# GpSimd adds the weighted expert rows of 23 mixtures, TensorE turns the sums with four transposes instead of eight

## The chip, the cores and the metric

The kernel runs on one core of a Trainium2 chip, in one launch. The metric is the device time of that core in microseconds. The reasoning below uses one profiled execution of the kernel before; how its time stands to the timed runs is in the table further down.

## What is computed

The input x has 64 sequences of 128 tokens with 256 channels; a context of the same length has 192 channels. In the reference, cut to what matters:

```python
x = x + xattn(layernorm(x), ctx)         # 16 heads of 64, softmax over 128 keys, projection with bias
h = layernorm(x)
probs = softmax(h @ gate_w.T)            # 8 experts
top2_w, top2_idx = top_k(probs, 2)
expert_out = silu(h @ expert_w[e].T + expert_b[e])         # for each expert e
mixed = sum over the token's two experts of top2_w * expert_out
x = x + mixed @ combine_w.T
```

All is float32. The change touches the sum in the line of `mixed`.

## The kernel before, in words

The 8192 tokens are 32 pairs of sequences, 256 tokens each. Time is laid out in slots, numbered s, eight to a pair (`SLOTS`); i = s // 8 is the pair and u = s % 8 the pair of heads that slot s works on. Each engine has its own loop over the slots (`for s, i, u in slots()`), and each executes its instructions strictly in the order written. The engines meet through semaphores.

Attention in one slot: TensorE turns the normalised probabilities of the head pair before (`turn_probs`, L607), makes queries and keys (`queries_keys`), then scores of the next head pair (`scores`), and after some general jobs `attend` and `project`, all through the helper `products` (L566), since each float32 product is three products of a high and a low part. ScalarE takes exponentials (`exps`, L828) and rounds PSUM results to their high parts (`split_hi`, L801). VectorE makes row maxima (L1008), sums and their inverses (L1015, L1017) and the low parts (L960). GpSimd splits the attended rows (`split_attended`, L1318 and L1320), normalises the probabilities by the inverse sums (`normalise_probs`, L1309), and does small work and the indirect DMAs (`scatter` L1328, `gather` L1341).

Experts: for the first 28 pairs (`SPARSE`) the tokens are sorted by expert in DRAM in five chunks. A block of 128 sorted rows is turned (`turn_block`, L690), multiplied by its expert's weights (`expert`) and stored to `sorted_y`. The last four pairs go through all experts after the attention phase (`dense`).

A mixture m is the last step for pair m. GpSimd gathers its four 128x256 row blocks (two tokens halves t by two experts k) into the buffer `got[m % 2]`, one indirect DMA each. At slot s in `plan.mix` ScalarE multiplies each block with its weights (`weigh`, L896). In slot s+1 TensorE runs the job `turn_mixed`: for each of the four 128x128 pieces of the result two transposes that accumulate in PSUM, so that the sum over the two experts is made there (`turn_sum`, L657). ScalarE and VectorE split the result (`mT_s`), and in slot s+2 TensorE multiplies it by the combining weights (`combine`). VectorE adds the kept x (L1037), and SyncE stores the result.

The order around the change is written out by `Plan`. In each slot TensorE does turn_probs, the early jobs (turn_block), queries_keys, scores, the mid jobs (value products, turning and gating of the pair, turn_mixed), attend, project, the late jobs (expert, combine). ScalarE does exps, pT, attended, tanh, early, qk, mid (where the high part of the turned mixture is taken), and last `weigh`. GpSimd does split_attended, normalise_probs, small work, scatter, gather. The attention phase is slots 0 to 255; a mixture is gathered over the two or four GpSimd slots just before it is weighed. Of the 28 mixtures of the sorted pairs, 23 are weighed at slots below 256; those before the end of attention stand at u = 7 and u = 1. The buffer `got` is free again when the turn of the mixture two before is made, which `gather` waits for.

The turn in `turn_sum` reads piece (t, k) of the buffer:

```python
for k in range(2):
    mm = pe.matmul(bank[:, a * N2 + t * P:a * N2 + (t + 1) * P],
                   src[:, 2 * t + k, a * P:(a + 1) * P], ident[:, :], is_transpose=True,
                   start=k == 0, stop=k == 1)
```

Of the kernel before, what the change touches and what calls it, by code (L numbers as in the profile page):

```python
# [5 lines left out]
P = 128  # L6
# [4 lines left out]
ALU = mybir.AluOpType  # L11
ACT = mybir.ActivationFunctionType
# [4 lines left out]
SLOTS = HEAD_PAIRS  # L17
# [38 lines left out]
class Plan:  # L56


    def __init__(self, pairs):
        self.ends = [sum(CHUNKS[:c + 1]) for c in range(len(CHUNKS))]  # L60
        self.blocks = [4 * n + 7 for n in CHUNKS]
        self.first = [sum(self.blocks[:c]) for c in range(len(CHUNKS))]
        self.chunk_of = [c for c, n in enumerate(CHUNKS) for _ in range(n)]

        self.turn, self.gather, self.mix = {}, {}, {}
        at = free = 0
        for c, end in enumerate(self.ends):
            at = max(at, SLOTS * (end + 1) + 6)
            for b in range(self.blocks[c]):
                self.turn[at] = (c, b, self.first[c] + b)  # L70
                at += 1
            free = max(free, at + 4)
            for m in range(end - CHUNKS[c], end):
                if m >= 2:
                    free = max(free, sorted(self.mix)[m - 2] + 1)
                for k in range(4):
                    while len(self.gather.get(free, [])) >= self.room(free, pairs):
                        free += 1
                    self.gather.setdefault(free, []).append((m, k))
                self.mix[max(free + 2, max(self.mix, default=0) + 2)] = m  # L80
                free += 1

        self.dense = {}
        at = SLOTS * pairs
        for n in range(DENSE_JOBS * (pairs - SPARSE)):
            m = SPARSE + n // DENSE_JOBS
            if n % DENSE_JOBS == 0:
                at = max(at, SLOTS * (m + 2))
            while len(self.dense.get(at, [])) >= (DENSE_PER_SLOT if at >= SLOTS * pairs + 2 else 2):
                at += 1  # L90
            self.dense.setdefault(at, []).append(n)
            if n % DENSE_JOBS == DENSE_JOBS - 1:
                free = at + 2
                while any(near in self.mix for near in (free - 1, free, free + 1)):
                    free += 1
                self.mix[free] = m

        self.pair_of = [self.mix[at] for at in sorted(self.mix)]
        self.turn_of = {m: r for r, m in enumerate(self.pair_of)}
        self.mix = {at: r for r, at in enumerate(sorted(self.mix))}  # L100
        self.last = max(max(self.turn) + 4, max(self.mix) + 4)
        self.jobs_at, order = {}, []
        for s in range(-SLOTS, self.last + 1):
            i, u = s // SLOTS, s % SLOTS
            early, mid, late = [], [], []
            for kind, k, off in ATTENTION_JOBS.get(u, []):
                if 0 <= i + off < (SPARSE if kind == "rank" else pairs):
                    mid.append((kind, (i + off) * per(kind) + k))
            if s in self.turn:
                early.append(("turn_block", self.turn[s][2]))  # L110
            if s - 1 in self.mix:
                mid.append(("turn_mixed", self.mix[s - 1]))
            if s - 1 in self.turn:
                late.append(("expert", self.turn[s - 1][2]))
            if s - 2 in self.mix:
                late.append(("combine", self.mix[s - 2]))
            self.jobs_at[s, "early"], self.jobs_at[s, "mid"], self.jobs_at[s, "late"] = early, mid, late
            order += early + mid + late
        self.place = {job: n for n, job in enumerate(order)}
        self.order = order  # L120
# [16 lines left out]
def xattn_moe_kernel(nc, x, ctxT, wq, wkv, wkv_rest, wproj, bproj, gateT, expertT, expert_b, combineT, out):  # L137
    pairs = x.shape[0] // (2 * P)
# [20 lines left out]
    with ExitStack() as stack:  # L159
# [3 lines left out]
        def sem(name):  # L163
            return stack.enter_context(nc.semaphore(name))
# [52 lines left out]
        def carve(n, rows):  # L217
# [117 lines left out]
            sem(n) for n in ("top_done", "route_step", "top_w_done", "hot_done", "rows_done", "blocks_done"))  # L335

        ctx_rest = sem("ctx_rest")
        ctx_lo, probs_done, weighted = (
            sem(n) for n in ("ctx_lo", "probs_done", "weighted"))
        eps_done = [sem(f"eps_done{n}") for n in (1, 2)]  # L340
        rstd_done = [sem(f"rstd_done{n}") for n in (1, 2)]

# [220 lines left out]
        def _(pe):  # L563
# [88 lines left out]
            def turn_sum(src, bank):  # L652

                for t in range(2):
                    for a in range(2):
                        for k in range(2):
                            mm = pe.matmul(bank[:, a * N2 + t * P:a * N2 + (t + 1) * P],  # L657
                                           src[:, 2 * t + k, a * P:(a + 1) * P], ident[:, :], is_transpose=True,
                                           start=k == 0, stop=k == 1)
                return mm  # L660

# [71 lines left out]
            def general(s, position):  # L733
                for kind, n in plan.jobs_at[s, position]:
                    if (before := plan.before_in_bank(kind, n)) is not None:
                        pe.wait_ge(drained[before[0]], before[1] + 1)
                    bank = gen_ps[plan.bank(kind, n)]
                    if kind == "value":
                        mm = value(n, bank)
                    elif kind == "turn_x":  # L740
                        pe.wait_ge(xn_done, n + 1)
                        mm = turn(x_raw, bank)
                    elif kind == "turn_x1":
                        pe.wait_ge(xn2_done, n + 1)
                        mm = turn(xn2[n % 2], bank)
                    elif kind == "gate":
                        mm = gate(n, bank)
                    elif kind == "rank":
                        mm = rank(n, bank)
                    elif kind == "turn_block":  # L750
                        mm = turn_block(n, bank)
                    elif kind == "expert":
                        mm = expert(n, bank)
                    elif kind == "turn_mixed" and plan.pair_of[n] < SPARSE:
                        m = plan.pair_of[n]
                        pe.wait_ge(weighted, m + 1)
                        mm = turn_sum(got[m % 2], bank)
                    elif kind == "turn_mixed":
                        m = plan.pair_of[n] - SPARSE
                        pe.wait_ge(dense_added, 2 * DENSE_JOBS * (m + 1))  # L760
                        mm = turn(acc[m], bank)
                    else:
                        mm = combine(n, bank)
                    mm.then_inc(made[kind], 1)
# [32 lines left out]
        def _(act):  # L797
# [94 lines left out]
            def weigh(m):  # L892
                act.wait_ge(gathered[m % 2], 64 * (m // 2 + 1))
                act.wait_ge(top_w_done, m + 1)
                for k in range(4):
                    last = act.activation(got[m % 2][:, k, :], got[m % 2][:, k, :], ACT.Copy, scale=top_w[:, m, k:k + 1])  # L896
                last.then_inc(weighted, 1)

            def gate_exps(j):
# [387 lines left out]
        def _(pool):  # L1287
# [18 lines left out]
            def normalise_probs(j, p):  # L1306
                pool.wait_ge(inv_done, j * HEAD_PAIRS + p + 1)
                b = p % 2
                pool.tensor_tensor(probs[b][:, :, :], probs[b][:, :, :],  # L1309
                                   inv_sums[b][:, :].unsqueeze(2).broadcast_to([P, 4, P]),  # L1310
                                   ALU.mult).then_inc(probs_done, 1)
# [20 lines left out]
            def gather(m, k):  # L1332
                c = plan.chunk_of[m]
                through = plan.first[c] + plan.blocks[c]
                if k == 0:
                    for r in range(RING):
                        pool.wait_ge(y_stored[r], 16 * blocks_in_ring(r, through))
                    pool.wait_ge(y_rows_done, c + 1)
                    if m >= 2:
                        pool.wait_ge(made["turn_mixed"], plan.turn_of[m - 2] + 1)  # L1340
                pool.indirect_dma_start(  # L1341
                    out=got[m % 2][:, k, :], out_offset=None, in_=sorted_y[c],
                    in_offset=bass.IndirectOffsetOnAxis(ap=y_row_of[:, m, k:k + 1], axis=0)).then_inc(
                        gathered[m % 2], 16)

            for b in range(AHEAD):
                pool.memset(k_s[b][:, :, :, :].bitcast(F32), 0.0)
# [19 lines left out]
            for s, i, u in slots():  # L1367
# [4 lines left out]
                    split_attended(i, u - 2)  # L1372
                if now:
                    normalise_probs(i, u)
                if s in (-SLOTS + 1, 1):
                    rsqrt(i + 1, 0)
                if u == 6 and i >= 0 and exists(i + 2):
# [52 lines left out]
```

## Time and profile before

| what | value |
|---|---|
| timed runs | 1630.62 us median of 3 (1629.04 to 1634.59) |
| the profiled execution | 1637.44 us |
| its span, first to last instruction | 1635.4 us |
| TensorE matmul / weight loads busy | 94% / 90% |
| VectorE, ScalarE, GpSimd busy | 77%, 65%, 54% |
| granted TensorE clock, mean | 0.989 of full |

All times of single instructions are from the profiled execution, in microseconds from the start of its span. Busy shares are averages over the whole span; a timeline row shows one instruction, or several alike merged, with its start and duration and, in brackets, the idle time of its engine before it. PE is TensorE, DVE VectorE, ACT ScalarE, POOL GpSimd, PEld TensorE's weight loads. The tile `stage` in the rows is the scratch buffer that holds `got`, the probabilities and more.

### The profile page before, as it was taken

How to read it: one execution, taken by the hardware profiler on the slowest of the kernel's cores; microseconds unless marked ns; L12 is line 12 of the kernel's file. 1: busy time of each engine (PE TensorE's matmuls, PEld its weight loads, DVE VectorE, ACT ScalarE, POOL GpSimd, SP SyncE). 2: the span in 40 equal slices, each digit the busy share in tenths (PEclk: the TensorE clock that was granted, in tenths of full speed). 3: DMA queues.
4: the chain of work that ended last, by engine and by line, in shares of the span. 5: the costliest groups of instructions: out<-in, count | busy, mean ns of one | idle time of the engine just before them, and what ended most of it. 6: DMA issues, size and time to landing. Idle time of an engine off the chain costs nothing.

```text
span 1635.4 us, 39352 instructions
## 1 busy us (share of the span) xinstructions
PE 1537.0 (94%) x11891; PEld 1470.2 (90%) x11891; DVE 1264.0 (77%) x3135; ACT 1062.0 (65%) x2890; POOL 879.9 (54%) x1185
## 2 busy tenths in 40 slices
PE   4999999998999999999999999999999999999787
PEld 4899999998999999998999999899998998999675
DVE  5788888777888888877877888877778787776566
ACT  4766666665666766675767667666766666666433
POOL 4655555555545555576655545575656465644410
PEclk9999999999999999999999999999999999999999
DMA  6633333333577777344677667467777776877722
GB/s 226 203 85 91 92 91 92 91 91 95 173 216 223 223 217 210 101 123 128 201 224 227 204 213 217 135 188 226 230 227 211 220 229 198 248 218 216 273 64 78
DMA packets 179131, 286.99 MB, mean 175 GB/s; under 512 B 23575, under 2 KB 113900, under 8 KB 178668
## 3 DMA queue, kind: packets, MB, share of 16 engines
q1 hardware_dynamic: 168172, 255.11, 52.7%
q0 software_dynamic: 10752, 29.37, 5.8%
q8 instruction: 99, 1.62, 0.4%
q14 instruction: 108, 0.88, 0.2%
HBM read 155.66 MB, written 61.62 MB: 133 GB/s over the span
## 4 chain that ended last, share of the span: by engine, by line
PE 73%; DVE 10%; issue 6%; ACT 5%; POOL 4%; DMA 1%; SPq 0%; ACTq 0%; DVEq 0%; POOLq 0%
PE gen_ps L566 21%; PE qk_ps L566 15%; PE o_ps L566 9%; PE proj_ps L566 9%; PE s_ps L566 8%; PE pT_ps L607 6%; ACT stage L801 2%; PE gen_ps L690 1%; PE gen_ps L657 1%; PE gen_ps L665 1%; DMA k_s<-qk_s 1%; DVE sums L1015 1%; ACT v_s_hi L801 1%; POOL sorted_x L1328 1%; POOL stage L1309 1%
## 5 line engine op out<-in xcount | busy, mean ns | idle before, releaser
L828 ACT ACTIVATE stage<-s_ps,neg_max 128x128 f32<-128x128 f32 x1024 | 292.8, 371 | 105.8 <-DVE neg_max L1008 95.7
L1318 POOL CAST o_s_hi<-stage 128x256 fp32r<-128x256 f32 x256 | 102.2, 399 | 477.0 <-ACT stage L801 471.8
L1309 POOL TENSOR_TENSOR stage<-stage,inv_sums 128x512 f32<-128x512 f32 x256 | 266.8, 1042 | 15.9 <-DVE inv_sums L1017 15.9
L801 ACT CAST pT_s_hi<-pT_ps 128x512 fp32r<-128x512 f32 x256 | 150.9, 589 | 150.9 <-PE pT_ps L607 141.8
L566 PE MATMUL s_ps<-k_s,qk_s 128*128 128x256 f32 x1536 | 226.6, 283 | 4.1 <-DMA k_s<-qk_s 3.2
L1015 DVE TENSOR_REDUCE sums<-stage 128x4 f32<-128x512 f32 x256 | 172.9, 676 | 66.5 <-ACT stage L828 56.7
L960 DVE TENSOR_TENSOR pT_s_lo<-pT_ps,pT_s_hi 128x512 fp32r<-128x512 f32 x256 | 172.8, 675 | 56.0 <-ACT pT_s_hi L801 50.3
L960 DVE TENSOR_TENSOR qk_s<-qk_ps,qk_s 128x512 fp32r<-128x512 f32 x256 | 175.8, 687 | 41.8 <-ACT qk_s L801 39.0
L566 PEld LDWEIGHTS s_ps<-k_s,qk_s 128*128 128x128 f32 x1536 | 201.4, 191 | 4.9 <-DMA k_s<-qk_s 3.9
L1320 POOL TENSOR_TENSOR o_s_lo<-stage,o_s_hi 128x256 fp32r<-128x256 f32 x256 | 188.0, 734 | 21.1
L801 ACT CAST v_s_hi<-gen_ps 128x512 fp32r<-128x512 f32 x129 | 75.7, 587 | 177.2 <-PE gen_ps L566 173.3
L801 ACT COPY stage<-o_ps 64x256 f32<-64x256 f32 x512 | 188.4, 368 | 3.1
L566 PE MATMUL qk_ps<-xT_hi,wq_s_hi 128*128 128x256 f32 x512 | 166.7, 326 | 11.4 <-DVE wkvr_s_lo L971 6.5
L566 PE MATMUL o_ps<-pT_s_hi,v_s_hi 128*128 128x256 f32 x512 | 156.0, 305 | 22.4 <-DVE pT_s_lo L960 19.2
L1008 DVE TENSOR_REDUCE neg_max<-s_ps 128x4 f32<-128x512 f32 x256 | 174.4, 681 | 2.5 <-PE s_ps L566 2.5
L801 ACT CAST qk_s<-qk_ps 128x512 fp32r<-128x512 f32 x256 | 152.8, 597 | 24.8 <-PE qk_ps L566 18.2
L566 PE MATMUL proj_ps<-wproj_s_hi,o_s_hi 128*128 128x256 f32 x512 | 149.5, 292 | 12.5 <-POOL o_s_lo L1320 12.5
L607 PE MATMUL pT_ps<-ident,stage 128*128 128x128 f32 x1024 | 156.9, 276 | 2.2 <-POOL stage L1309 1.0
L566 PE MATMUL o_ps<-pT_s_lo,v_s_hi 128*128 128x256 f32 x512 | 145.2, 284 | 0.0
L566 PE MATMUL o_ps<-pT_s_hi,v_s_lo 128*128 128x256 f32 x512 | 145.2, 284 | 0.0
L566 PE MATMUL qk_ps<-xT_lo,wq_s_hi 128*128 128x256 f32 x512 | 144.5, 282 | 0.0
L566 PE MATMUL proj_ps<-wproj_s_hi,o_s_lo 128*128 128x256 f32 x512 | 143.9, 281 | 0.0
(358 smaller groups left out, 4706.1 us busy)
## 6 DMA issues: line engine op xcount, KB each, us to landing
w_block<-expert_table SPq DMA_DIRECT2D x147, 512.0 KB
k_s<-qk_s SPq DMA_DIRECT2D x512, 128.0 KB
stage<-sorted_x SPq DMA_DIRECT2D x147, 128.0 KB
sorted_y<-stage SPq DMA_DIRECT2D x147, 128.0 KB
x_raw<-in_x SPq DMA_DIRECT2D x32, 256.0 KB
c_raw<-in_ctxT SPq DMA_DIRECT2D x32, 256.0 KB, 3.3
stage<-in_x SPq DMA_DIRECT2D x32, 256.0 KB
x_kept<-x SPq DMA_DIRECT2D x32, 256.0 KB
```

Of the source, the lines that this page charges most:

```text
L566: mm = pe.matmul(out_ap, l, r, start=start and n == 0, stop=stop and n == len(terms) - 1, skip_group_check=skip)
L607: mm = pe.transpose(pT_ps[:, k * P:(k + 1) * P], probs[p % 2][:, k, :], ident[:, :])
L657: mm = pe.matmul(bank[:, a * N2 + t * P:a * N2 + (t + 1) * P], src[:, 2 * t + k, a * P:(a + 1) * P], ident[:, :], is_transpose=True, start ...
L665: mm = pe.transpose(bank[:, a * N2 + t * P:a * N2 + (t + 1) * P], src[:, t, a * P:(a + 1) * P], ident[:, :])
L801: last = act.copy(to, of)
L828: last = act.activation(probs[p % 2][:, k, :], s_ps[:, k * P:(k + 1) * P], ACT.Exp, bias=neg_max[p % 2][:, k:k + 1])
L960: last = dve.tensor_tensor(lo, of, hi.bitcast(F32), ALU.subtract)
L1008: dve.tensor_reduce(neg_max[p % 2][:, :], s_ps[:, :].rearrange("p (k n) -> p k n", k=4), AX_X, ALU.max, negate=True).then_inc(max_done, 1)
L1015: dve.tensor_reduce(sums[p % 2][:, :], probs[p % 2][:, :, :], AX_X, ALU.add).then_inc(sums_done, 1)
L1309: pool.tensor_tensor(probs[b][:, :, :], probs[b][:, :, :], inv_sums[b][:, :].unsqueeze(2).broadcast_to([P, 4, P]), ALU.mult).then_inc(prob ...
L1318: pool.tensor_copy(hi[:, :, :], o_full).then_inc(o_hi, 1)
L1320: pool.tensor_tensor(lo[:, :, :], o_full, hi[:, :, :].bitcast(F32), ALU.subtract).then_inc(o_lo, 1)
```

## The change

GpSimd adds, for the 23 mixtures weighed below slot 256, the two experts' weighted rows of each token, in one instruction over 128 partitions and 512 columns, in place, and raises the new semaphore `rows_added`. TensorE's turn_mixed for these mixtures waits for `rows_added` in place of `weighted` and uses the plain `turn` (L665 before, four transposes). The add stands in GpSimd's slot s+1, behind normalise_probs. The four gathered blocks lie in a new order in the buffer, so that the first experts' blocks of both halves are neighbours, and the second experts' too; the gather, the weighing and `turn_sum` follow that order. The other five mixtures of sorted pairs, and the four of the dense pairs, are turned as before.

```diff
+        early = [m for at, m in sorted(self.mix.items()) if at < SLOTS * pairs]
+        self.added_first = {m: n for n, m in enumerate(early)}
...
@@ turn_sum
-                                           src[:, 2 * t + k, a * P:(a + 1) * P], ident[:, :], is_transpose=True,
+                                           src[:, t + 2 * k, a * P:(a + 1) * P], ident[:, :], is_transpose=True,
...
@@ general, TensorE
-                        pe.wait_ge(weighted, m + 1)
-                        mm = turn_sum(got[m % 2], bank)
+                        if m in plan.added_first:
+                            pe.wait_ge(rows_added, plan.added_first[m] + 1)
+                            mm = turn(got[m % 2][:, 0:2, :], bank)
+                        else:
+                            pe.wait_ge(weighted, m + 1)
+                            mm = turn_sum(got[m % 2], bank)
...
@@ weigh, ScalarE
-                    last = act.activation(got[m % 2][:, k, :], got[m % 2][:, k, :], ACT.Copy, scale=top_w[:, m, k:k + 1])
+                    last = act.activation(got[m % 2][:, k // 2 + 2 * (k % 2), :], got[m % 2][:, k // 2 + 2 * (k % 2), :], ACT.Copy,
+                                          scale=top_w[:, m, k:k + 1])
...
@@ gather, GpSimd
-                    out=got[m % 2][:, k, :], out_offset=None, in_=sorted_y[c],
+                    out=got[m % 2][:, k // 2 + 2 * (k % 2), :], out_offset=None, in_=sorted_y[c],
...
+            def add_rows(m):
+
+                pool.wait_ge(weighted, m + 1)
+                first, second = (got[m % 2][:, k:k + 2, :].rearrange("p t c -> p (t c)") for k in (0, 2))
+                pool.tensor_tensor(first, first, second, ALU.add).then_inc(rows_added, 1)
...
@@ the loop over the slots, GpSimd
                 if now:
                     normalise_probs(i, u)
+                if s - 1 in plan.mix and plan.pair_of[plan.mix[s - 1]] in plan.added_first:
+                    add_rows(plan.pair_of[plan.mix[s - 1]])
                 if s in (-SLOTS + 1, 1):
                     rsqrt(i + 1, 0)
```

## Rows read from the trace of the kernel before

**Rows 1.** The page: busy time by engine, and the chain by engine.
```profile
PE 1537.0 (94%) x11891; PEld 1470.2 (90%) x11891; DVE 1264.0 (77%) x3135; ACT 1062.0 (65%) x2890; POOL 879.9 (54%) x1185
...
PE 73%; DVE 10%; issue 6%; ACT 5%; POOL 4%; DMA 1%; SPq 0%; ACTq 0%; DVEq 0%; POOLq 0%
```

**Rows 2.** Timeline of TensorE in slot 200: start, duration, engine, line, operation.
```profile
1156.25 1.03 PE L657 MATMUL gen_ps<-ident,stage 128*128 128x128 f32 x8
```

**Rows 3.** Timeline of GpSimd in slots 200 and 201.
```profile
1157.24 1.04 POOL L1309 TENSOR_TENSOR stage<-stage,inv_sums 128x512 f32<-128x512 f32 x1
1158.43 1.06 POOL L1328 DMA_INDIRECT sorted_x<-xn,row_of  x1 [0.16 <-issue]
1161.37 0.39 POOL L1318 CAST o_s_hi<-stage 128x256 fp32r<-128x256 f32 x1 [1.88 <-ACT stage L801]
```

**Rows 4.** Timeline of TensorE in slots 130, 202, 216 and 256.
```profile
728.56 1.03 PE L657 MATMUL gen_ps<-ident,stage 128*128 128x128 f32 x8
...
1171.82 1.03 PE L657 MATMUL gen_ps<-ident,stage 128*128 128x128 f32 x8
...
1265.91 0.43 PE L566 MATMUL o_ps<-pT_s_hi,v_s_hi 128*128 128x256 f32 x1 [2.56 <-DVE pT_s_lo L960]
...
1522.41 1.04 PE L657 MATMUL gen_ps<-ident,stage 128*128 128x128 f32 x8
1523.82 0.38 PE L566 MATMUL o_ps<-pT_s_hi,v_s_hi 128*128 128x256 f32 x1 [0.37 <-issue]
```

**Rows 5.** Timeline of GpSimd in slots 130, 202, 203, 216 and 256.
```profile
728.12 1.04 POOL L1309 TENSOR_TENSOR stage<-stage,inv_sums 128x512 f32<-128x512 f32 x1
...
1170.28 1.03 POOL L1309 TENSOR_TENSOR stage<-stage,inv_sums 128x512 f32<-128x512 f32 x1
1175.28 0.20 POOL L1302 TENSOR_TENSOR var_eps<-mv,eps 128x2 f32<-128x2 f32 x1 [3.97 <-DVE mv L984]
...
1265.36 1.04 POOL L1309 TENSOR_TENSOR stage<-stage,inv_sums 128x512 f32<-128x512 f32 x1 [1.98 <-DVE inv_sums L1017]
...
1524.22 0.74 POOL L1320 TENSOR_TENSOR o_s_lo<-stage,o_s_hi 128x256 fp32r<-128x256 f32 x1
```

**Rows 6.** Chain of waits in slots 200, 201, 216: start, length, what.
```profile
1156.41 0.87 PE gen_ps L657 x8
1157.29 0.71 PE o_ps L566 x6
...
1159.54 0.44 PE pT_ps L607 x4
...
1265.87 0.04 issue
1265.91 1.50 PE o_ps L566 x6
```

**Rows 7.** Single lines' instructions: count, nanoseconds least/median/most, first and last start.
```profile
L657 PE MATMUL gen_ps<-ident,stage x224: 270/272/474, 715.9 to 1617.6; 128*128 128x128 f32 x112
...
L1291 POOL TENSOR_TENSOR w_block<-stage,w_block x8: 1275/1293/1478, 33.7 to 68.4; 128x512 fp32r<-128x512 f32 x8
```

**Rows 8.** Timeline of ScalarE in slots 200 and 201.
```profile
1157.38 0.59 ACT L801 CAST mT_s_hi<-gen_ps 128x512 fp32r<-128x512 f32 x1 [0.22 <-PE gen_ps L657]
1158.69 1.14 ACT L828 ACTIVATE stage<-s_ps,neg_max 128x128 f32<-128x128 f32 x4 [0.73 <-DVE neg_max L1008]
```

**Rows 9.** Stretches: length, busy time by engine, granted TensorE clock, DMA share, GB/s.
```profile
1263.40:1265.90 2.50, 0.00 (x0) 0.00 (x0) 2.36 (x10) 0.59 (x1) 0.54 (x1) 1.00 0.02 5
1266.50:1269.40 2.90, 2.90 (x16) 2.90 (x15) 2.52 (x7) 1.14 (x4) 1.06 (x1) 0.50 0.43 138
1613.30:1615.30 2.00, 0.00 (x0) 0.00 (x0) 1.96 (x5) 2.00 (x5) 0.00 (x0) 1.00 0.45 131
1615.40:1619.30 3.90, 2.49 (x20) 2.25 (x20) 2.77 (x5) 0.61 (x2) 0.00 (x0) 1.00 0.15 54
713.40:1521.70 808.30, 776.12 (x6174) 751.33 (x6175) 628.57 (x1574) 543.19 (x1510) 458.33 (x604) 0.99 0.70 208
```

More of the change, by code:

```diff
@@ L337, in xattn_moe_kernel @@
         ctx_rest = sem("ctx_rest")
-        ctx_lo, probs_done, weighted = (
-            sem(n) for n in ("ctx_lo", "probs_done", "weighted"))
+        ctx_lo, probs_done, weighted, rows_added = (
+            sem(n) for n in ("ctx_lo", "probs_done", "weighted", "rows_added"))
         eps_done = [sem(f"eps_done{n}") for n in (1, 2)]
```

## The prediction

> **What bounds the kernel now.** I read the page first, then the groups by line, then the timelines of single slots and the chain of waits. The page gives TensorE 94% of the span and GpSimd 54%; the chain that ended last runs 73% through TensorE and 4% through GpSimd [rows 1]. So work taken from TensorE in the attention phase is worth its full time there, and GpSimd has room on average. Whether it has room at the moment in question is another matter, and only a timeline tells.
>
> A mixture weighed by ScalarE in slot s is turned by TensorE in slot s+1. I number slots as the kernel does; 23 mixtures have s under 256. By the plan their turns fall into slots with u = 0 (12 of them: 128, 136, 144, 152, 192, 200, 208, 216, 232, 240, 248, 256) and u = 2 (11: the slot two behind each of these but the last). Slot 200 is a typical u = 0. There TensorE starts the eight turns at 1156.25 [rows 2], while GpSimd is still splitting; its normalisation of the same slot's probabilities runs from 1157.24 to 1158.28 [rows 3]. In a u = 2 slot TensorE has a value product ahead of the turn and comes later: in slot 202 it turns at 1171.82, and the normalisation ended at 1171.31 [rows 4, 5].
>
> **The change, step by step.**
>
> *Turns.* The eight transposes stand in the chain with 0.87 us, four probability transposes of the same shape with 0.44 [rows 6]. Four fewer save 0.43 us, and 23 x 0.43 = 9.9 us is all that the change can give. (The 272 ns of a single one [rows 7] overlap with the next and must not be summed.)
>
> *The add.* Nothing in the trace is this add. The nearest row is a 128x512 subtraction with two full inputs on GpSimd, 1293 ns in the median of 8 and 1478 at most [rows 7]; from below the normalisation, 128x512 with a broadcast second input, 1.04 us [rows 3]. I take 1.29, the shape and inputs being the same, and keep 1.04 and 1.48 as ends. The Trainium skill, "GPSIMD Engine Reference", section on elementwise cycle accounting, gives 4497 ns for such an add of 2048 columns and holds that elementwise work is better left to VectorE; a quarter of that is 1.12 us, an estimate, and with it the sum below would be some 4 us smaller. No run here shows the add yet.
>
> *Its place.* GpSimd executes in order and the add stands right behind the normalisation of its slot. Its own inputs are ready long before (the weighing was done before that slot's exponentials), so it starts 0.03 us before the normalisation is recorded as ended, and TensorE follows some 0.05 after its end (such a step between engines is 0.04 on the chain [rows 6]): turns start at normalisation end + 1.31 us. That new wait is the heart of the matter.
>
> *Slots with u = 0, eight alike* (128, 144, 152, 192, 200, 208, 240, 248). In slot 200: 1158.28 + 1.31 = 1159.59 instead of 1156.25, 3.34 us late [rows 2, 3], less 0.43 is 2.9. Over the eight I read 3.24 to 3.51 in the same way, mean 3.37, net 2.94: 23.5 us. Behind the waiting turn on TensorE are attend, project, the expert block and the whole next slot. In slots 200 and 201 there is no idle time in which to win it back. On ScalarE the rounding of the turned sums stands ahead of the next exponentials: it ended at 1157.97 and the exponentials began at 1158.69 [rows 8], so they slip too, and VectorE and GpSimd behind them. All four engines are held by one wait, and nobody runs ahead.
>
> *Slots 136, 216, 232* (u = 0 at a chunk's end). VectorE is busy with the list of blocks, and attend already waited: in slot 216 it began at 1265.91 [rows 4]. The normalisation ended at 1266.40 [rows 5]; turns at 1267.71, attend 0.44 later at 1268.15, 2.2 us later than now. Three of them: 6.7 us.
>
> *Slot 256* has no normalisation. The split ended at 1524.96 [rows 5], the add 1.26 later, turns at 1526.27, attend at 1526.70 instead of 1523.82 [rows 4]: 2.9 us. The gather behind it on GpSimd waits for this turn as well and slips by less than that.
>
> *Slots with u = 2.* Slot 202: 1171.31 + 1.31 - 1171.82 = 0.80, less 0.43: 0.37 us. Nine alike: 3.3. Slots 130 and 138 have no expert block's transposes ahead: 729.16 + 1.31 - 728.56 = 1.91, net 1.48 [rows 4, 5]; two: 3.0.
>
> *GpSimd itself.* 23 x 1.29 = 30 us more, hidden: in slot 200 it next splits at 1161.37, 3.1 us after the normalisation [rows 3]; in slot 202 it idles from 1171.31 to 1175.28 until VectorE's statistics come [rows 5]. One scatter issue of 1.06 us moves back into that room [rows 3]. Were the cover gone, each add would delay the next split by up to 1.3 us. ScalarE's weighing and the gathers only change which rows they address: nothing.
>
> Waits net of saved turns: 23.5 + 6.7 + 2.9 + 3.3 + 3.0 = 39.4 us.
>
> *The clock.* TensorE idles in each u = 0 slot for 3.2 us (1156.41 [rows 6] to 1159.59). In the trace an idle stretch of that size is followed by a stretch at half clock (1.2 instead of 2.4 GHz): after TensorE's idle 1263.4 to 1265.9 the granted clock is 0.50 for some 3 us, while an idle 2.0 us near 1614 leaves it at 1.00 [rows 9]. All eight idle stretches from 2.45 us up, the start aside, did this, and none below 2.2. The price is in slot 216: six attend matmuls cost 1.50 us on the chain instead of 0.71 [rows 6], projection and expert lose 0.57 and 0.42 likewise, 1.8 us in all. Nine new falls (eight alike and slot 256) cost 9 x 1.8 = 16 us; slots 136, 216 and 232 pay it already.
>
> Sum: 39.4 + 16 = 55 us. The profiled execution took 1637.4 us (span 1635.4), 6.8 above the median of the runs, 1630.6. On the median: 1630.6 + 55 = 1686.
>
> **Rivals.**
>
> *No fall of the clock.* If the new idle stretches do not bring it down, because they are cut by the few matmuls around them, only the waits stand: 1630.6 + 39 = 1670. For it: 3.2 us lies within, not above, the stretches that show a fall. Against it: 2.5 us was enough in slot 216 [rows 9]. Chance 0.23.
>
> *A longer cold stretch.* Around 765 the low clock lasted twice as long as elsewhere; if wait and fall meet so in most of the twelve slots, some 1.8 x 12 = 21 us come on top: 1707. Chance 0.10.
>
> *Recovered waits.* TensorE has 808 - 776 = 32 us of idle time between 713 and 1522 us [rows 9]. If the other engines use the stall to get ahead, up to that much returns: near 1654. Against it stands ScalarE's place behind the same turn. Chance 0.09.
>
> *Faster.* If the sum is there before TensorE asks, the change gives its 9.9 us: 1621. The place is the turn, the price the end of the add against the start of the turn; it decides once the normalisation ends 1.31 us before the turn. In u = 2 it ends 0.51 before, in u = 0 2.03 after, so none of the 23 qualifies. It needs the timeline to be wrong by microseconds. Chance 0.03, with 0.02 for something that cancels out.
>
> *It doesn't do what it says.* The four rows are gathered to new places, first rows in halves 0 and 1, second in 2 and 3, so one add yields the sums that four transposes turn; the later mixtures keep their eight. I see no way in which the adds fail to happen.
>
> **How the numbers follow.** My forecast with the clock's fall has 0.53, giving 1686, with the add's ends (23 x 0.25 less, 23 x 0.19 more) 1680 to 1691. The range reaches down to the recovered waits and up toward the long cold: 1653 to 1706. A measurement of this kernel tells some 0.3%, 5 us, from no change. Slower has 0.95, same 0.02, faster 0.03.
>
> **What would show it.** In the profile after: 23 adds of 128x512 on GpSimd at about 1.29 us; the 224 transposes of sums cut to 92 in fours and 40 in eights; TensorE before the four-fold turns idle on GpSimd, some 3.2 us in u = 0 and 0.8 in u = 2, 45 to 55 us in all; ScalarE's rounding of the turned sums waiting as long; a mean granted clock a little lower, with half-clock stretches behind the u = 0 turns. I am wrong if that wait is a few microseconds in total, or if the stall is there and the following slots are shorter by it.

## The result, and the profile after

The changed kernel took 1689.5 us in the median of 4 runs (1684.2 to 1691.0), the kernel before, run beside it, 1632.6. The ratio is 1.0346 with a 95% interval of 1.0322 to 1.0369: slower by 57 us, where 1686 in a range of 1653 to 1706 was forecast. The profiled execution is the fastest of the four, 1684.2 us, with a span of 1682.4.

The page of the kernel after, the lines that answer to [rows 1]:

```profile
PE 1541.0 (92%) x11799; PEld 1470.5 (87%) x11799; DVE 1264.8 (75%) x3135; ACT 1059.5 (63%) x2890; POOL 906.0 (54%) x1208
...
PE 67%; POOL 9%; ACT 8%; DVE 8%; issue 7%; DMA 1%; ACTq 0%; SPq 0%; POOLq 0%; DVEq 0%
```

TensorE executes 92 matmuls fewer, as it should, and is yet busy 4 us longer: a part of its work ran at a lower clock. In the chain that ended last its share fell from 73% to 67%, and GpSimd's rose from 4% to 9%. The totals of waits say on what TensorE waited, and the single line says how long the add takes (ns, least/median/most):

```profile
PE gen_ps L668 <- POOL stage L1358: 55.1, 23, 5.7
PE proj_ps L569 <- POOL o_s_lo L1328: 12.5, 17, 1.0
PE o_ps L569 <- DVE pT_s_lo L968: 11.6, 16, 3.7
```
```profile
L1358 POOL TENSOR_TENSOR stage<-stage x23: 1257/1262/1273, 714.6 to 1571.5; 128x512 f32<-128x512 f32 x23
```

23 waits of the turn (L668) for the add (L1358), 55.1 us together, the longest 5.7: this wait did not exist before, and it heads the list by far. Slot 200, the timeline of TensorE after, answers to [rows 2]:

```profile
1175.38 0.88 PE L569 MATMUL s_ps<-k_s,qk_s 128*128 128x256 f32 x6
1179.37 0.63 PE L668 MATMUL gen_ps<-ident,stage 128*128 128x128 f32 x4 [3.11 <-POOL stage L1358]
1179.75 0.36 PE L569 MATMUL o_ps<-pT_s_hi,v_s_hi 128*128 128x256 f32 x1
```

and that of GpSimd, to [rows 3]:

```profile
1176.28 0.73 POOL L1328 TENSOR_TENSOR o_s_lo<-stage,o_s_hi 128x256 fp32r<-128x256 f32 x1
1176.96 1.04 POOL L1317 TENSOR_TENSOR stage<-stage,inv_sums 128x512 f32<-128x512 f32 x1
1177.96 1.26 POOL L1358 TENSOR_TENSOR stage<-stage 128x512 f32<-128x512 f32 x1
1179.38 1.05 POOL L1336 DMA_INDIRECT sorted_x<-xn,row_of  x1 [0.15 <-issue]
```

Split, normalisation and add stand one behind the other on GpSimd, and TensorE, which has ended its scores, takes up the turn 0.15 us after the add. ScalarE is held behind it, as the timeline of ScalarE shows (see [rows 8]):

```profile
1180.09 0.59 ACT L808 CAST mT_s_hi<-gen_ps 128x512 fp32r<-128x512 f32 x1 [3.19 <-issue]
1180.57 1.15 ACT L835 ACTIVATE stage<-s_ps,neg_max 128x128 f32<-128x128 f32 x4
```

In slot 202 (u = 2) the wait is short, compare [rows 4]:

```profile
1196.96 0.63 PE L668 MATMUL gen_ps<-ident,stage 128*128 128x128 f32 x4 [0.71 <-POOL stage L1358]
```

The clock in slots 200 and 201, in stretches as in [rows 9], and then the same stretch of the chain, as in [rows 6]:

```profile
1176.30:1179.30 3.00, 0.00 (x0) 0.00 (x0) 1.95 (x4) 0.60 (x2) 2.92 (x3) 1.00 0.86 233
1179.40:1181.50 2.10, 2.10 (x15) 2.10 (x16) 0.76 (x2) 1.41 (x5) 1.03 (x1) 0.74 0.82 271
1181.50:1184.50 3.00, 3.00 (x18) 3.00 (x18) 1.02 (x3) 0.41 (x2) 0.00 (x0) 0.61 0.17 57
1185.50:1188.00 2.50, 2.50 (x18) 2.28 (x18) 1.88 (x5) 1.46 (x5) 2.15 (x4) 1.00 0.80 294
```
```profile
1179.37 0.63 PE gen_ps L668 x4
1180.00 0.84 PE o_ps L569 x6
1180.84 1.28 PE proj_ps L569 x6
1182.12 1.49 PE gen_ps L569 x7
```

TensorE is idle for 3 us, then the granted clock falls to 1.2 GHz for a few microseconds, and projection and expert block take 1.28 and 1.49 us where at 2.4 GHz they take 0.71 and 0.83. The slot, from one turn of the probabilities to the next, grew from 5.76 to 9.95 us.

Measured in this way in both profiles, the eight like slots with u = 0 grew by 4.0 to 4.5 us each, 34 in all, and the slots behind them by 1 in all; the three chunk ends by 2.6 to 2.9, net of the slots behind them 8; nine slots with u = 2 by 0.45 each and slots 130 and 138 by 1.57, together 7. In slot 256 the turn waited 3.7 us, and TensorE's next long idle stretch begins 21.0 us after that slot's turn of the probabilities instead of 17.0: 4 more. That makes 54. The two profiled executions are only 47 us apart (spans of 1682.4 and 1635.4), since that of the kernel before is 6.8 us above its median and that of the kernel after the fastest of its four. The 7 us between stand where the change does nothing, half of them ahead of slot 128 or in slots that it leaves alone, half in the dense pairs, where in the profile after the clock stayed at 1.00 behind two idle stretches of 3.0 us that were each followed by a fall in the profile before. So a difference of a few microseconds between two single profiles says nothing by itself; below I go by slots.

### The profile page after: what moved, and what is told of

The parts are those of the page before. It is cut to its first block, busy times and chain, and to the rows that moved or that the text cites. A ratio compares the mean times of both kernels' runs of the same rounds, so it can differ in the third digit from the quotient of the medians.

```text
span 1682.4 us, 39191 instructions
## 1 busy us (share of the span) xinstructions
PE 1541.0 (92%) x11799; PEld 1470.5 (87%) x11799; DVE 1264.8 (75%) x3135; ACT 1059.5 (63%) x2890; POOL 906.0 (54%) x1208
## 4 chain that ended last, share of the span: by engine, by line
PE 67%; POOL 9%; ACT 8%; DVE 8%; issue 7%; DMA 1%; ACTq 0%; SPq 0%; POOLq 0%; DVEq 0%
PE gen_ps L569 19%; PE qk_ps L569 13%; PE proj_ps L569 9%; PE o_ps L569 9%; PE s_ps L569 7%; PE pT_ps L610 6%; ACT stage L808 3%; POOL stage L1317 2%; PE gen_ps L668 2%; POOL o_s_lo L1328 2%; POOL stage L1358 2%; PE gen_ps L693 1%; POOL o_s_hi L1326 1%; ACT stage L903 1%; ACT stage L835 1%
## 5 line engine op out<-in xcount | busy, mean ns | idle before, releaser
L569 PE MATMUL proj_ps<-wproj_s_lo,o_s_hi 128*128 128x256 f32 x512 | 146.6, 286 | 0.0
```

The source lines that it names most:

```text
L569: mm = pe.matmul(out_ap, l, r, start=start and n == 0, stop=stop and n == len(terms) - 1, skip_group_check=skip)
```

## The experiments

All ratios are to the kernel before, run on the same chip in the same comparison, 1630.4 to 1631.0 us there. "Worth x us" is a ratio times 1631.

**Four transposes without the add (e1, and again e10).**

```diff
-                            pe.wait_ge(rows_added, plan.added_first[m] + 1)
+                            pe.wait_ge(weighted, m + 1)
                             mm = turn(got[m % 2][:, 0:2, :], bank)
...
-                if s - 1 in plan.mix and plan.pair_of[plan.mix[s - 1]] in plan.added_first:
-                    add_rows(plan.pair_of[plan.mix[s - 1]])
```

> No add is made; TensorE turns only the first experts' rows of the 23 mixtures with four transposes and waits for the weighing as before, so the second experts' share is left out of them. Theory (the loss is TensorE's wait for the add, the saving is real): 4 x 23 transposes at 0.11 us come off the bound engine, 1632.6 - 9.9 = 1623 us. Rival (transposes were hidden, so nothing could be gained): 1632 to 1633.

Measured: 1626.9 us, ratio 0.9971 (0.9955 to 0.9988). The saving is real but half of what was expected, 4.7 us instead of 9.9. Since that is my term of the sum that the trace seemed to give most directly, it was run again:

> The same kernel as the first run (four transposes, no add, the second experts' share left out), timed again with more rounds, because it gained 0.29% with an interval from 0.12% to 0.45%, where 9.9 us would be 0.6%. If each four transposes are worth their whole 0.43 us: ratio 0.994. If part is given back in the slot behind, where projection then waits for GpSimd's split (0.15 us in the u = 3 slots of that run): 9.9 - 11 x 0.15, less the three chunk ends (1.3), 7 us, ratio 0.9957. If more is lost elsewhere: 0.997 or above.

Measured: 1627.6 us, ratio 0.9973 (0.9955 to 0.9991), 4.4 us. Both intervals exclude 9.9 us; both hold 7, at their edge. Slot by slot the profile of the first run shows where it goes. The u = 2 slots are shorter by 0.44 each, seven of the eight like u = 0 slots by 0.31 to 0.43 and slot 128 by 0.08, but nine of the eleven u = 3 slots are longer by 0.14 to 0.18. Together that is 6.2 us without the chunk ends, in the profile of e10 as well, and 6.2 lies within both intervals. In the u = 3 slots TensorE has come nearer to GpSimd. The timeline of TensorE in slot 203 of that run, then GpSimd's:

```profile
1171.06 0.28 PE L569 MATMUL o_ps<-pT_s_hi,v_s_lo 128*128 128x256 f32 x1
1171.41 0.38 PE L569 MATMUL proj_ps<-wproj_s_hi,o_s_hi 128*128 128x256 f32 x1
```
```profile
1169.05 1.07 POOL L1336 DMA_INDIRECT sorted_x<-xn,row_of  x1 [0.20 <-issue]
1170.13 0.41 POOL L1326 CAST o_s_hi<-stage 128x256 fp32r<-128x256 f32 x1
1170.62 0.74 POOL L1328 TENSOR_TENSOR o_s_lo<-stage,o_s_hi 128x256 fp32r<-128x256 f32 x1
```

Projection starts 0.35 us after the last attend matmul, where 0.12 is the usual step, since GpSimd's split ends at 1171.36, held back by the scatter before it. In slots 216 and 232 attend waits for VectorE in any case.

**Sixteen transposes (e11)**, the price from the other side.

```diff
-                            pe.wait_ge(rows_added, plan.added_first[m] + 1)
-                            mm = turn(got[m % 2][:, 0:2, :], bank)
+                            pe.wait_ge(weighted, m + 1)
+                            turn_sum(got[m % 2], bank)
+                            mm = turn_sum(got[m % 2], bank)
```

and no add, as above.

> The kernel before with the eight transposes of each of the 23 mixtures made twice (16), no add. The price of transposes from the other side: 8 more are 0.87 us on the chain. If TensorE is the bound in all 23 slots: 23 x 0.87 = 20 us, ratio 1.0123. Where VectorE holds the slot (three chunk ends) or others absorb some: 17 us, 1.0104. If each transpose is worth only the half that the first run showed: 10 us, 1.006.

Measured: 1648.1 us, ratio 1.0103 (1.0082 to 1.0124), 17 us for 184 transposes more, as expected where three chunk ends absorb theirs. By slots the eight more cost 0.83 to 0.89 us in each like slot and each slot with u = 2. So a transpose added costs its 0.11 us, and one removed gives less: on the side of removal the next limit is near.

**The wait with all eight transposes (e2).**

```diff
                             pe.wait_ge(rows_added, plan.added_first[m] + 1)
-                            mm = turn(got[m % 2][:, 0:2, :], bank)
+                            mm = turn_sum(got[m % 2], bank)
```

> As the changed kernel, add and wait in place, but TensorE keeps its eight accumulating transposes, so the second experts' rows count twice in these mixtures. Theory: the wait costs the same and the saving is gone, 1689.5 + 9.9 = 1699 us, with the same idle before the turns (about 55 us). Rival (the stall ends on something other than the add, so the transposes fit into it): 1690.

Measured: 1699.8 us, ratio 1.042 (1.0392 to 1.0447), 12 us above the changed kernel by the ratios and 10 by the times. TensorE's totals of waits in that run:

```profile
PE gen_ps L660 <- POOL stage L1358: 55.9, 23, 6.0
```

The same wait, 55.9 us against 55.1, and four transposes more behind each. Behind such a wait the four transposes are worth their whole 0.43 us: nine slots with u = 2 are 0.89 to 0.92 us longer than in the kernel before, where in the changed kernel they were 0.45 longer. The price of the wait is therefore not 57 but 67 to 69 us, of which the change gives 10 to 12 back.

One slot of this run bears on the clock. Slot 192, the turn and the stretch behind it:

```profile
1130.63 1.06 PE L660 MATMUL gen_ps<-ident,stage 128*128 128x128 f32 x8 [3.27 <-POOL stage L1358]
1130.70:1133.70 3.00, 3.00 (x27) 3.00 (x27) 1.17 (x4) 1.63 (x5) 0.99 (x1) 1.00 0.53 150
```

TensorE idled 3.27 us and the clock did not fall. The slot is 3.5 us longer than before, the other seven like slots of the run, each with a fall, are 4.6 to 6.1 longer. So the fall is likely behind such a wait, and not certain.

**The stall filled (e3)**, to tell the idle time from the clock.

```diff
+                            if s % SLOTS == 0:
+                                for _ in range(24):
+                                    pe.transpose(bank[:, 0:P], ident[:, :], ident[:, :])
                             pe.wait_ge(rows_added, plan.added_first[m] + 1)
                             mm = turn(got[m % 2][:, 0:2, :], bank)
```

> As the changed kernel, but in slots with u = 0 TensorE turns the identity 24 times (24 x 0.11 = 2.7 us) into the bank ahead of its wait; the bank is written over afterwards. The stall of 3.2 us stays, only filled. Theory (some 16 us of the loss are the half clock that follows the idle stretches): the granted clock stays at 1.00 behind the eight alike slots and slot 256, 1689.5 - 16 = 1673 us. Rival (the clock costs nothing because TensorE waits anyway): 1689, or a little more.

Measured: 1670.3 us, ratio 1.025 (1.0222 to 1.0277); against the changed kernel 0.0096 of ratio, 16 us. The filling and the stretch behind it in slot 200 of that run, timeline and stretches:

```profile
1171.30 2.78 PE L762 MATMUL gen_ps<-ident 128*128 128x128 f32 x24
1174.48 0.65 PE L668 MATMUL gen_ps<-ident,stage 128*128 128x128 f32 x4 [0.40 <-POOL stage L1361]
```
```profile
1174.50:1180.50 6.00, 6.00 (x49) 5.91 (x50) 3.11 (x8) 3.98 (x11) 2.24 (x4) 1.00 0.58 163
```

TensorE does useless work for 2.8 us, waits 0.4 for the same add, and the clock stays at 2.4 GHz behind it; the mean granted clock over the run is 0.993 against 0.982. The rival that had the clock cost nothing is out: 16 us hang on it, give or take some 6 by the two intervals, and 41 us of the loss stay when it is kept up. By slots the split is finer. The eight like slots are 2.8 to 3.1 us longer than before in this run, mean 2.95, where they were 4.0 to 4.5 longer, mean 4.30, in the changed kernel: the clock's fall costs 1.35 us in each, and some 0.13 in the slot behind, 12 us for the eight. Slot 256 gives 1.5 more by the measure used above. The rest stands at the chunk ends, which are shorter than in the changed kernel by 1.0 to 2.3 us. There the kernel before had its falls already, but in slots 216 and 232 of the changed kernel the slow stretch lasts twice as long. Slot 216 of the changed kernel:

```profile
1297.40:1300.40 3.00, 3.00 (x15) 3.00 (x16) 1.15 (x4) 1.63 (x5) 1.00 (x1) 0.50 0.62 146
1300.40:1303.20 2.80, 2.80 (x15) 2.80 (x15) 0.64 (x2) 0.00 (x0) 0.00 (x0) 0.50 0.84 311
```

With the filling, one of the three chunk ends has no fall and two have a short one. How much of this part is the change's and how much an old loss cannot be told apart: chunk ends that are made alike differ by as much from run to run (see e5).

**Only the u = 2 mixtures added (e5).**

```diff
-        early = [m for at, m in sorted(self.mix.items()) if at < SLOTS * pairs]
+        early = [m for at, m in sorted(self.mix.items()) if at < SLOTS * pairs and at % SLOTS == 1]
```

> The changed kernel, but only the 11 mixtures turned in slots with u = 2 are added on GpSimd; the 12 of u = 0 are turned with eight transposes, as before. Theory (the wait is the end of the add against TensorE's arrival, 0.7 us in nine of these slots and 1.8 in two): 9 x 0.4 + 2 x 1.5 = 6.6 us over the kernel before, which ran at 1631 in the last comparison: 1638 us. Nearly all of the 55 us belongs to u = 0. Rival (each add costs alike, 55 / 23 = 2.4 us): 1657 us.

Measured: 1640.1 us, ratio 1.0048 (1.0032 to 1.0063), 8 us, with 10.0 us of TensorE's waits for the add. Adds do not cost alike: the same instruction costs 0.7 us in one place and 4 in another. By subtraction, the twelve of u = 0 carry the other 49.

This run also makes its chunk ends as the kernel before does, and shows what a fall alone costs. Slot 216, where TensorE idled 2.50 us ahead of attend (2.56 in the kernel before [rows 4]), the stretch behind:

```profile
1270.10:1273.10 3.00, 3.00 (x26) 3.00 (x27) 2.63 (x8) 1.22 (x5) 1.40 (x2) 1.00 0.50 162
```

The clock stayed at 2.4 GHz, and the slot took 8.55 us instead of the 10.10 of the profile before, where it fell [rows 9]. The three chunk ends with the slots behind them are 3.0 us shorter here than in that profile, and 2.9 in e8, though nothing was changed in them. All differences at chunk ends that I give are to that slower profile.

**A second instruction before the release (e6).**

```diff
-                pool.tensor_tensor(first, first, second, ALU.add).then_inc(rows_added, 1)
+                pool.tensor_tensor(first, first, second, ALU.add)
+                pool.tensor_tensor(second, second, second, ALU.add).then_inc(rows_added, 1)
```

> The changed kernel, but GpSimd makes a second instruction of the same size (it doubles the second experts' rows, which nobody reads any more) before it releases TensorE. Theory: every wait grows by one add, 23 x 1.27 = 29 us, from 1689.5 to 1719, or somewhat more if the clock falls in slots with u = 2 too, where the idle time grows from 0.7 to 2.0 us. Rival (something later than the add ends the wait, or the stall is won back): under 1700.

Measured: 1720.0 us, ratio 1.054 (1.0521 to 1.056), 32 us above the changed kernel. The second instruction and TensorE's wait, from the views of its line and of the waits:

```profile
L1359 POOL TENSOR_TENSOR stage<-stage x23: 1032/1038/1042, 717.7 to 1607.8; 128x512 f32<-128x512 f32 x23
```
```profile
PE gen_ps L668 <- POOL stage L1359: 78.3, 23, 6.7
```

It has the same tile as both inputs and takes 1.04 us, not 1.27. The wait grew by 78.3 - 55.1 = 23.2 us, 1.01 for each; the time grew by some 8 more, and the mean clock fell from 0.982 to 0.968. Slots 194 and 202 (both u = 2) show what these 8 us are: the turn, then the stretch behind it.

```profile
1155.89 0.63 PE L668 MATMUL gen_ps<-ident,stage 128*128 128x128 f32 x4 [1.71 <-POOL stage L1359]
1155.90:1158.90 3.00, 3.00 (x26) 3.00 (x27) 1.60 (x5) 1.63 (x5) 0.00 (x0) 1.00 0.82 234
1216.80 1.09 PE L668 MATMUL gen_ps<-ident,stage 128*128 128x128 f32 x4 [1.71 <-POOL stage L1359]
1216.80:1219.80 3.00, 3.00 (x14) 3.00 (x15) 1.20 (x3) 1.63 (x5) 0.00 (x0) 0.50 0.82 223
```

After the same idle 1.71 us the clock stayed up in one and fell in the other. Of the nine slots with u = 2 that idle so, five fell and are 2.7 to 2.8 us longer than before, the four others 1.46; of slots 130 and 138 one fell. These six falls are 7.6 us, less 1.4 that the slots behind gave back.

**The add at the head of GpSimd's slot (e4).**

```diff
                 now, before, nxt = exists(i), exists(i - 1), exists(i + 1)
+                if s - 1 in plan.mix and plan.pair_of[plan.mix[s - 1]] in plan.added_first:
+                    add_rows(plan.pair_of[plan.mix[s - 1]])
                 if u < 2 and before:
                     split_attended(i - 1, 6 + u)
...
                 if now:
                     normalise_probs(i, u)
-                if s - 1 in plan.mix and plan.pair_of[plan.mix[s - 1]] in plan.added_first:
-                    add_rows(plan.pair_of[plan.mix[s - 1]])
```

> As the changed kernel, but the add stands at the head of GpSimd's slot s+1, before the split and the normalisation. In slots with u = 0 it would run from about 1155.3 to 1156.5 in the times of the kernel before, where TensorE asks at 1156.25; in u = 2 GpSimd idles there for 4 us. Theory (only the add's place behind the normalisation costs): wait 0.35 us in eight slots, none in u = 2, 23 x 0.43 saved, some 1.5 us lost in slot 256: 1628 us, between 1624 and 1632. Rival (an add on GpSimd costs by itself, by delaying splits and normalisations): over 1640.

Measured: 1636.4 us, ratio 1.0036 (1.0022 to 1.005). Moving three lines takes away 51 of the 57 us, which puts the loss on the place of the add and not on the add. TensorE's waits for it:

```profile
PE gen_ps L668 <- POOL stage L1358: 4.8, 10, 1.2
```

But it is 6 us slower than before and not 3 faster. By slots in the profiles, the u = 2 ones gain their 0.44 us. Slot 128 loses 1.0 us with a wait of 1.2. Of the chunk ends, slot 216 with the one behind it loses 2.3 and slot 232 loses 1.3, although their turns wait 0.16 and 0.14 us. The cause is on VectorE. The add on GpSimd in slot 216, the instruction of VectorE beside it, TensorE's attend, and the same instruction of VectorE in the kernel before:

```profile
1258.75 1.31 POOL L1358 TENSOR_TENSOR stage<-stage 128x512 f32<-128x512 f32 x1
1258.23 1.88 DVE L1169 TENSOR_TENSOR_SCAN rows_to<-rows_new,zeros 128x9 f32<-128x9 f32 x1
1264.91 0.58 PE L569 MATMUL o_ps<-pT_s_hi,v_s_hi 128*128 128x256 f32 x1 [4.08 <-DVE pT_s_lo L968]
```
```profile
L1161 DVE TENSOR_TENSOR_SCAN rows_to<-rows_new,zeros x5: 178/178/182, 396.1 to 1363.5; 128x9 f32<-128x9 f32 x5
```

A step of VectorE's list of blocks that takes 0.18 us took 1.88, until GpSimd's add was done. The same happened in slot 232 (1.86 us) and, with the step two further on, in slot 136 (1.95). So the list ends later, and attend, which waits for VectorE there, starts 1.4, 1.4 and 2.0 us later in these slots than before. Stretches of slot 216 in that run:

```profile
1262.00:1264.50 2.50, 0.00 (x0) 0.00 (x0) 2.33 (x11) 0.00 (x0) 0.14 (x1) 0.76 0.00 0
1265.00:1268.00 3.00, 3.00 (x14) 3.00 (x15) 2.62 (x8) 1.14 (x4) 1.45 (x2) 0.50 0.52 164
1268.00:1271.00 3.00, 3.00 (x20) 3.00 (x19) 0.89 (x3) 0.72 (x2) 0.00 (x0) 0.64 0.71 215
```

TensorE also idles longer before attend, 4.1 us instead of 2.6; the clock falls while it still idles and stays low behind it for most of 6 us, where the kernel before had some 3 [rows 9]. That this longer slow stretch is the rest of slot 216's loss fits, but no run tested it by itself.

**Head of the slot, u = 2 only (e8).** The two edits of e4 and e5 together.

> The add at the head of GpSimd's slot, and only for the 11 mixtures turned in slots with u = 2, where GpSimd idles for some 4 us; the 12 of u = 0 are turned with eight transposes as before. Theory: no wait anywhere, 11 x 0.44 us saved, about 0.15 given back in the slot behind as the run with the add at the head showed: 1631 - 3 = 1628 us. Rival (the saving is lost in the next slot): 1631.

Measured: 1630.8 us, ratio 0.9994 (0.9985 to 1.0003). No gain that can be told from nothing; the 3 us expected would be 0.998, just outside the interval.

**The add on VectorE (e7).**

```diff
+            def add_rows(m):
+                dve.wait_ge(weighted, m + 1)
+                first, second = (got[m % 2][:, k:k + 2, :].rearrange("p t c -> p (t c)") for k in (0, 2))
+                dve.tensor_tensor(first, first, second, ALU.add).then_inc(rows_added, 1)
...
                 now, before, nxt = exists(i), exists(i - 1), exists(i + 1)
+                if s - 1 in plan.mix and plan.pair_of[plan.mix[s - 1]] in plan.added_first:
+                    add_rows(plan.pair_of[plan.mix[s - 1]])
                 if now:
                     inverse(i, u)
```

and GpSimd's call of `add_rows` is gone.

> The add is made by VectorE instead of GpSimd, at the head of its slot s+1, ahead of the row sums, for all 23. There VectorE idles about 1 us while ScalarE takes the exponentials, and such an add should take it 0.7 us. Theory (the saving is real where the wait is hidden): no wait of TensorE in 20 slots; the three slots at a chunk's end, where VectorE is late anyway, lose 0.7 us each. The run with four transposes and no add gained 5 us, so 1631 - 5 + 2 = 1628 us, between 1622 and 1633. Rival (VectorE has no room, each add delays the sums by 0.7 us): 1631 - 5 + 16 = 1642.

Measured: 1629.1 us, ratio 0.9992 (0.9979 to 1.0005). TensorE's wait for it, from the view of waits:

```profile
PE gen_ps L668 <- DVE stage L1230: 8.1, 3, 3.1
```

Three waits, those of the chunk ends; in the other 20 slots none. That names the next step:

**The add on VectorE, chunk ends left out (e9).**

```diff
-        early = [m for at, m in sorted(self.mix.items()) if at < SLOTS * pairs]
+        early = [m for at, m in sorted(self.mix.items())
+                 if at < SLOTS * pairs and not (at % SLOTS == 7 and at // SLOTS in self.ends)]
```

> As the run with the add on VectorE, but the three mixtures turned at a chunk's end (slots 136, 216, 232), where VectorE makes the list of blocks and its add came late, keep eight transposes. Theory: these three adds each cost VectorE 0.7 us on the path (2 us in all) and give nothing, so 1629 - 2 = 1627 us, a ratio to the kernel before of 0.9975. Rival (nothing to gain there): 0.999.

Measured: 1624.0 us, ratio 0.996 (0.9937 to 0.9983), a gain of 6 us over the kernel before (3 to 10 by the interval), and the fastest version with the full computation. Its adds, from the view of the line:

```profile
L1231 DVE TENSOR_TENSOR stage<-stage x20: 682/693/693, 711.2 to 1509.8; 128x512 f32<-128x512 f32 x20
```

0.69 us each, in time that VectorE spent waiting for the exponentials (0.9 to 1.9 us in these slots of the kernel before; behind the add it still waits 0.3 or more), and nobody waits for them.

## Why the prediction was right, point by point

- *The wait for the add, 39.4 us net.* Right: e3 leaves 41 us when the clock is kept up, and the eight like slots are 2.95 us longer there, against 2.94 forecast. In slots with u = 2 it is 0.45 against 0.37 in nine, and 1.57 against 1.48 in two, and in slot 256 2.4 (e3) against 2.9. At the three chunk ends attend starts 2.5 to 2.6 us later, against 2.2.
- *Its cause, the place behind the normalisation.* Shown by e4, where the same add a few instructions earlier costs 6 us instead of 57, by e5 for the split by u, and by e6 for the slope. e4 also shows a price that the prediction did not have: an add of GpSimd beside VectorE's list of blocks holds VectorE up.
- *The clock, 16 us for nine falls.* The mechanism was right, the term a little large: 1.35 us in each like slot and 0.13 behind it instead of 1.8, some 13 us for nine; e3 as a whole shows 16, but a part of that belongs to the chunk ends. That eight of eight idle stretches from 2.45 us up brought a fall, and none below 2.2, held in the one trace it was read from, and not in others: slot 192 of e2 idled 3.27 us without a fall, slot 216 of e5 2.50 without one, and in e6 1.71 us were enough in five slots of nine. All nine new idle stretches of the changed kernel's profile were followed by a fall, so the count came true, but it was a likelihood and not a rule. The fall comes somewhat after the stall, during attend, so attend's first matmuls still run at 2.4 GHz; in slot 216 of before, from which the 1.8 was taken, it came at once.
- *The add, 1.29 us.* 1.26. The rows with two full inputs were the right ones, against the 1.04 with a broadcast input. The 1.12 that the prediction estimated is a quarter of the 4497 ns that the Trainium skill, "GPSIMD Engine Reference", section "Elementwise — side-by-side cycle accounting", gives for an add of 2048 columns. The trace of the kernel before has an instruction of that size, a subtraction, which agrees (4547 ns), but a quarter of the columns takes more than a quarter of the time (1262 ns):

```profile
L1291 POOL TENSOR_TENSOR wproj_s_lo<-stage,wproj_s_hi x1: 4547/4547/4547, 24.2 to 24.2; 128x2048 fp32r<-128x2048 f32 x1
```

- *Release to start, 0.05 us.* Wrong by 0.1: TensorE starts 0.14 to 0.15 us after GpSimd's add ends, in all 23 places. That is 2 us, of which the shorter add (23 x 0.03) takes back 0.7, and it is the 0.08 by which the u = 2 slots came out longer.
- *The saving, 9.9 us.* Right in the place where it counted, behind the wait: 10 to 12 us by e2 against the changed kernel. But the sentence that TensorE's work in the attention phase "is worth its full time there" is wrong for the kernel without the wait, where e1 and e10 gave 4.7 and 4.4 us. The give-back to GpSimd's split in u = 3 slots is seen (nine times 0.15 us, 1.4 in all), and the chunk ends give nothing for three of the 23; by slots that leaves 6.2 in both profiles without the chunk ends, and what is lacking to the timed 4.4 and 4.7 is within the intervals.
- *Recovered waits.* Did not come: the slots behind the eight like stalls were as long as before, or by up to 0.3 us longer. Rounding the turned sums stands ahead of the exponentials on ScalarE, as forecast, and holds the other engines.
- *A longer cold stretch.* Came in two places, slots 216 and 232, where the slow stretch lasted twice as long as before; it did not in the eight like slots.
- *The sum.* By slots the terms come to 54 us against 55, and single ones are off by more and cancel: the eight like slots with those behind them 2.5 below the forecast, slot 256 0.8 below, the chunk ends 1.4 above, the slots with u = 2 0.6 above. That the total lies so close is in part luck.
- *Faster.* Its condition, a sum that is there before TensorE asks, was made by e7 and e9. Then the change does gain, 6 us at best, and not the 9.9 of that rival.

## What to carry to other kernels

Work given to an engine with room on average costs whatever the receiving end waits at the moment of need: compare the end of the new instruction, at its place in its engine's order, with the time at which its reader asks, slot by slot. If the reader is the bound engine and idles so long that its clock may fall, add the price of the slow stretch behind it; a few useless matmuls in the gap show that part by itself. Look also at what the other engines' instructions beside the new one take, since one of them may be held up by it, as VectorE was in e4. Look then for the engine that idles just before the need, here VectorE ahead of its row sums, before giving the idea up.

## What the runs showed of the hardware that was not expected

An elementwise instruction of GpSimd with the same 128x512 tile as both inputs took 1.038 us, the one with two different tiles 1.266 in the same run (e6), and the normalisation with a broadcast second input 1.04. And the step from the end of GpSimd's add to TensorE's first matmul was 0.14 to 0.15 us, more than three times the 0.04 read behind VectorE from the chain. It belongs to this release and not to GpSimd as such: in the same profile TensorE started 0.05 us after GpSimd's split and after its normalisation wherever it waited for them. Why is not known.

A step of VectorE on 128x9 took 1.9 us instead of 0.2 where a GpSimd instruction with two full 128x512 inputs ran beside it, in three chunk ends of three (e4).

Whether the granted clock falls after an idle stretch is not settled by its length: 1.71 us were followed by a fall in five slots of nine (e6), 2.50 us were not (e5), and 3.27 us were not (e2). A fall that came cost 1.3 to 1.6 us where TensorE was the bound.
